# Decoder block in float32: attention's maxima and exponentials head by head, and the last batch's output bias on GpSimd

## The chip, the cores and the metric

The kernel runs on one core of a Trainium2 chip. The metric is the device time of one execution in microseconds (us). The kernel before has a median of 809.09 us over three runs (807.49 to 811.71). The engines are PE (TensorE), DVE (VectorE), ACT (ScalarE), POOL (GpSimd) and SP (SyncE, which only issues DMAs here).

## The reference

Input `x` is 4 batches of 512 tokens by 512 features. Three pre-norm layers follow, each added to its input:

```
x = x + attention(layernorm(x))     # 16 heads of 32, window of 128 keys, 4 sink keys
x = x + experts(layernorm(x), ids)  # 4 experts picked by token id
x = x + ffn(layernorm(x))           # ternary weights, 8-bit activations
# attention, per head:
scores = q @ k.T * HEAD_DIM ** -0.5, -inf where (j >= 4) & (j < i - 128)
probs  = softmax(scores)
out    = (probs @ v) @ Wo.T + bo
```

Only attention is touched by the change. There is no causal mask: a query row sees the sink keys, the 128 keys before it and all keys after it.

## The kernel before

Three phases run one after the other, with a barrier of all engines between them: attention (to about 456 us), experts (to about 600 us), feed-forward (to the end).

In attention the 16 heads go in 4 groups of 4 (`GH` = 4), the queries of a batch in 4 tiles of 128. A **unit** is one head group `g` of one query tile `qt`, written (g,qt) here; there are 64. The units of group 0 of the next batch are numbered (4,qt), so the program runs (0,0) to (0,3) of batch 0, then for each batch (1,0) to (4,3), and for the last batch (1,0) to (3,3). Every unit needs:

- scores of 4 heads, each in a bank of its own of `s_ps`, 512, 512, 388 or 260 keys wide for `qt` = 0 to 3 (L902), and for `qt` > 0 a matmul per head that adds the window's mask (L910). They wait until all four exponentials of the unit before are done, since they overwrite `s_ps`
- the negated maximum of each head's row, on DVE (`maxima`, L696): two instructions for two heads each
- the exponentials with their row sums, on ACT (`exps`, L527): one instruction per head
- four "slots" of transposes on PE (L930; L926 for the sink columns; L923 for the widened reciprocals of the sums in `qt` = 3). Slots 0 and 2 are copied out of PSUM by ACT (L539), slots 1 and 3 by DVE (L717, L714). There is one PSUM bank for each of the two engines, so slot 2 waits for ACT's copy of slot 0, and slot 3 for DVE's copy of slot 1
- after each second unit the product with V (`attend_pair`, L952, L944).

Every engine has its order written out by hand (`unit` of each engine). In unit u, PE first computes the scores of unit u+1, then slots 0 and 1 of u, then a piece of "side" work (12 matmuls of 512 columns, L843: a tile of the next Q, K, V or of the output projection), then slots 2 and 3. DVE in unit u takes the maxima of u+1, then copies slot 1, does its part of the side work, and copies slot 3. ACT copies slot 0, takes the exponentials of u+1, copies slot 2. In the last batch there is no side work left after group 1, except three pieces of output projection in (3,2) and (3,3).

POOL widens the reciprocals (`widen`, L391), splits the group's result into two parts (`split`, L399 and L402), loads the residual `xres`, adds the bias `bo` to it (`add_bo`, L443, one instruction of 2048 columns after `split(b, 2)`), and in the last batch splits the experts' weights (`expert_hi` L431, `expert_lo` L437). In the last batch DVE adds `bo`, in four instructions of 512 columns (L768) at the ends of the units of `BO_UNITS`: (2,1), (2,2), (2,3), (3,0).

## Time and profile before

| | before |
|---|---|
| three runs | 807.49, 809.09, 811.71 us |
| profiled execution | 808.96 us, of which the span of its instructions is 807.1 us |
| busy over the span | PE 92%, DVE 73%, ACT 59%, POOL 35% |
| instructions in all | 14098 |
| maxima (L696) on DVE | 128 instructions, 124.5 us |
| exponentials (L527) on ACT | 256 instructions, 152.3 us, and 52.8 us of accumulator reads |

A busy share is the time in which the engine had an instruction under way; an engine can be idle much of the time and still be the one that others wait for in a given stretch. "Idle before" an instruction is the gap on its engine, with the instruction that ended it.

### The profile page before, as it was taken

Reading aid. Unit: us, or ns where it says so; the run is one execution under the profiler, and the core shown is the slowest. Engines: PE = TensorE matmul, PEld = TensorE weight load, DVE = VectorE, ACT = ScalarE, POOL = GpSimd, SP = SyncE. Lnnn points to the kernel's source line nnn. Section 1 sums busy time; section 2 is a strip of 40 time slices with the busy share of each in tenths; the row PEclk is TensorE's granted clock in tenths of the full one; section 3 lists DMA queues with packets and bytes.
Section 4 is the critical chain, followed back from the end, with each engine's and each line's share of the span. In section 5 each row is a group of like instructions: output and inputs, shape, how many; then the busy total and the mean of one; then the engine's idle time right before and its main releaser. Section 6 shows DMA issues by size and latency. Waiting matters only on the chain. (4 is left out here: it accounts for less than half of the span.)

```text
span 807.1 us, 14098 instructions
## 1 busy us (share of the span) xinstructions
PE 740.2 (92%) x5150; PEld 507.8 (63%) x5150; DVE 590.4 (73%) x1092; ACT 473.2 (59%) x1025; POOL 281.0 (35%) x282
## 2 busy tenths in 40 slices
PE   5988999999999999999978789999957899999997
PEld 4756777777777777777655568888833343434443
DVE  6886666877668866677675467778628888888875
ACT  5555676666666666677555144444415766767674
POOL 2011213223042130314455234443214555555552
PEclk9998999999999999999989899999989999999999
DMA  9200031113121040313210375553122232433332
GB/s 312 107 1 28 27 105 37 45 54 131 52 81 54 28 157 27 106 30 129 105 53 2 95 274 176 201 199 137 46 82 85 52 85 73 105 91 73 73 78 79
DMA packets 56482, 74.12 MB, mean 92 GB/s; under 512 B 35615, under 2 KB 37663, under 8 KB 54752
## 3 DMA queue, kind: packets, MB, share of 16 engines
q1 hardware_dynamic: 50672, 56.17, 22.8%
q0 software_dynamic: 5456, 16.53, 5.9%
q8 instruction: 43, 0.70, 0.4%
q10 hardware_dynamic: 288, 0.52, 0.2%
q14 instruction: 23, 0.19, 0.1%
HBM read 52.71 MB, written 13.39 MB: 82 GB/s over the span
## 5 line engine op out<-in xcount | busy, mean ns | idle before, releaser
L527 ACT ACTIVATE probs<-s_ps,neg_max 128x512 f32<-128x512 f32 (+2 forms) x256 | 152.3, 610 | 19.5 <-DVE neg_max L696 18.1
L696 DVE TENSOR_REDUCE neg_max<-s_ps 128x2 f32<-128x1024 f32 (+2 forms) x128 | 124.5, 1014 | 33.6 <-PE s_ps L910 33.0
L930 PE MATMUL pT_ps<-ident,probs 128*128 128x128 f32 x832 | 115.6, 280 | 9.7 <-DVE probs L717 8.4
L539 ACT ACTIVATE probs<-pT_ps 128x512 f32<-128x512 f32 x96 | 57.4, 598 | 98.6 <-PE pT_ps L930 98.3
L930 PEld LDWEIGHTS pT_ps<-ident,probs 128*128 128x128 f32 x832 | 93.9, 144 | 25.2 <-DVE probs L717 11.2
L717 DVE COPY probs<-pT_ps 128x512 f32<-128x512 f32 x112 | 76.6, 684 | 36.8 <-PE pT_ps L930 36.5
L1473 POOL TENSOR_TENSOR hw<-h,ln_w_sb 128x512 f32<-128x512 f32 x64 | 83.2, 1310 | 52.3 <-DVE h L1606 52.3
L1738 PE MATMUL f_y_ps<-w_tern,hqT 128*128 128x512 bf16 x256 | 65.1, 379 | 11.8 <-DVE xn L1648 5.3
L1717 PE MATMUL gate_ps<-w_tern,xqT 128*128 128x512 bf16 x256 | 65.9, 380 | 8.3 <-DVE h L1606 7.4
L843 PE MATMUL side_ps<-w_hi 128*128 128x512 f32 x172 | 71.0, 413 | 0.0
L843 PE MATMUL side_ps<-w_hi,w_lo 128*128 128x512 f32 x172 | 67.3, 391 | 0.0
L843 PE MATMUL side_ps<-w_lo,w_hi 128*128 128x512 f32 x172 | 67.2, 391 | 0.0
L1717 PE MATMUL up_ps<-w_tern,xqT 128*128 128x512 bf16 x256 | 65.7, 379 | 0.0
L399 POOL TENSOR_TENSOR aT_hi<-norm,one_col 128x512 fp32r<-128x512 f32 x15 | 15.6, 1040 | 125.0 <-DVE norm L708 86.6
L1606 DVE SCALAR_TENSOR_TENSOR h<-up_ps,gu_scale,f_gate 128x512 f32<-128x512 f32 x64 | 47.7, 745 | 7.1 <-ACT f_gate L1529 7.0
L527 ACT ACTIVATION_READ_ACCUMULATOR probs<-s_ps,neg_max 128x1 f32 x256 | 52.8, 206 | 0.0
L952 PE MATMUL pv_ps<-probs,v_sb 128*32 128x256 f32 (+1 forms) x896 | 52.3, 369 | 0.2 <-ACT probs L539 0.2
L391 POOL TENSOR_TENSOR norm<-rinv,one_col 128x512 f32<-128x512 f32 x16 | 16.7, 1041 | 102.8 <-DVE rinv L703 102.8
L1717 PEld LDWEIGHTS gate_ps<-w_tern,xqT 128*128 128x128 bf16 x256 | 23.6, 98 | 42.0 <-DVE h L1606 15.4
L1738 PEld LDWEIGHTS f_y_ps<-w_tern,hqT 128*128 128x128 bf16 x256 | 23.2, 97 | 42.0 <-DMA hqT<-hq 18.0
L1522 ACT ACTIVATE hq<-hq_big,minus_offset 128x1024 bf16<-128x1024 f16 x30 | 34.3, 1143 | 25.4 <-DVE hq_big L1643 25.4
L1529 ACT ACTIVATE f_gate<-gate_ps,gu_scale 128x512 f32<-128x512 f32 x64 | 43.1, 674 | 8.2 <-PE gate_ps L1717 8.2
(247 smaller groups left out, 1635.5 us busy)
## 6 DMA issues: line engine op xcount, KB each, us to landing
w_piece<-w_ffn SPq DMA_DIRECT2D x24, 512.0 KB
w_stage<-w_ffn SPq DMA_DIRECT2D x12, 1024.0 KB
xres<-x POOLq DMA_DIRECT2D x4, 1024.0 KB, 5.7
xn<-x SPq DMA_DIRECT2D x12, 256.0 KB, 3.0
xn<-x SPq DMA_DIRECT2D x3, 1024.0 KB
x<-xres POOLq DMA_DIRECT2D x3, 1024.0 KB, 4.8
xn<-c SPq DMA_DIRECT2D x2, 1024.0 KB, 6.1
v_next<-c SPq DMA_DIRECT2D x2, 1024.0 KB, 6.0
```

The source lines that it names most:

```text
L527: nc.scalar.activation(weights[qt][:, h, at:at + width(qt)], s_ps[:, h, 0:width(qt)], ACT.Exp, bias=neg_max[:, qt % 2, h:h + 1], accum_out ...
L539: nc.scalar.activation(out, turned_p, ACT.Identity).then_inc(slot_copied[0], 1)
L696: nc.vector.tensor_reduce(neg_max[:, qt % 2, 2 * s:2 * s + 2], s_ps[:, 2 * s:2 * s + 2, 0:width(qt)], AX.X, ALU.max, negate=True).then_inc ...
L717: nc.vector.tensor_copy(weights[qt][:, :, a:z], pT_ps[:, 1, :].rearrange("p (h n) -> p h n", h=GH))\
L843: last = nc.tensor.matmul(out, lt, r, start=(first and n == 0), stop=(final and n == len(terms) - 1))
L930: last = nc.tensor.transpose(pT_ps[:, k % 2, h * P:h * P + P], weights[qt][:, h, a:z], ident[:])
L952: last = nc.tensor.matmul(pv_ps[HD * h:HD * h + HD, to], v_sb[:, slot, f:f + HD], p, start=first, stop=final, tile_position=(0, HD * h))
L1473: nc.gpsimd.tensor_tensor(hw[:, t % 2, c, :], h[:, t % 2, c, :], ln_w[:, c * CHK:c * CHK + CHK], ALU.mult)\
L1529: nc.scalar.activation(gate[:, c % 2, :], gate_ps[c % 2][:], ACT.Silu, scale=gu_scale[:, t % 2, 0:1])\
L1606: nc.vector.scalar_tensor_tensor(h[:, i, c, :], up_ps[c % 2][:], gu_scale[:, i, 1:2], gate[:, c % 2, :], ALU.mult, ALU.mult).then_inc(h_re ...
L1717: last = nc.tensor.matmul(out[:], xqT[:, t % 2, k, :], weights[:, k, cols], start=(k == 0), stop=(k == DK - 1))
L1738: last = nc.tensor.matmul(y_ps[:], hqT[:, t % 2, k, :], down_w[:, k, :], start=(k == 0), stop=(k == FK - 1))
```

## The change

`maxima` issues four instructions for one head each instead of two for two heads, and each waits for its own head's scores; PE signals after every head; each exponential waits for its own head's maximum. In the last batch the bias is added on POOL by one instruction of 2048 columns between `widen(b, 2)` and `split(b, 2)`, and DVE's four additions go.

```
-BO_UNITS = [(2, 1), (2, 2), (2, 3), (3, 0)]
...
                 widen(b, 2)
+                add_bo(b)
                 split(b, 2)
...
-                def exps(b, g, qt, s):
-                    act.wait_ge(max_ready, units_before(b, g, qt) * 2 + s + 1)
+                def exps(b, g, qt):
                     at = BAND - width(qt) if qt >= 2 else 0
-                    for h in (2 * s, 2 * s + 1):
+                    for h in range(GH):
+                        act.wait_ge(max_ready, units_before(b, g, qt) * GH + h + 1)
                         nc.scalar.activation(weights[qt][:, h, at:at + width(qt)], s_ps[:, h, 0:width(qt)], ACT.Exp,
...
-                def maxima(b, g, qt, s):
-                    dve.wait_ge(scores_ready, units_before(b, g, qt) * 2 + s + 1)
-                    nc.vector.tensor_reduce(neg_max[:, qt % 2, 2 * s:2 * s + 2], s_ps[:, 2 * s:2 * s + 2, 0:width(qt)],
-                                            AX.X, ALU.max, negate=True).then_inc(max_ready, 1)
+                def maxima(b, g, qt):
+                    for h in range(GH):
+                        dve.wait_ge(scores_ready, units_before(b, g, qt) * GH + h + 1)
+                        nc.vector.tensor_reduce(neg_max[:, qt % 2, h:h + 1], s_ps[:, h, 0:width(qt)], AX.X, ALU.max, negate=True)\
+                            .then_inc(max_ready, 1)
...
-                    if last and (g, qt) in BO_UNITS:
-                        t = BO_UNITS.index((g, qt))
-                        if t == 0:
-                            dve.wait_ge(xres_loaded, (b + 1) * 16)
-                        nc.vector.tensor_tensor(xres[:, t, :], xres[:, t, :], bo_sb[:], ALU.add).then_inc(bo_added, 1)
...
                                                     start=(n == 0), stop=(n == 2 and not masked), tile_position=(HD * h, 0))
+                            if n == 2 and not masked:
+                                last.then_inc(scores_ready, 1)
                     if not masked:
-                        last.then_inc(scores_ready, 2)
                         return
...
                     for h in range(GH):
-                        last = nc.tensor.matmul(s_ps[:, h, at + free:at + P], ident_bf[:], window_mask[:, free:P], start=False, stop=True)
-                        if h % 2:
-                            last.then_inc(scores_ready, 1)
+                        nc.tensor.matmul(s_ps[:, h, at + free:at + P], ident_bf[:], window_mask[:, free:P], start=False, stop=True)\
+                            .then_inc(scores_ready, 1)
```

The callers call `maxima` and `exps` once instead of twice.

DVE in the last batch, from the end of unit (2,0) to the middle of (2,3), before (`neg_max` are the maxima, `probs<-pT_ps` a slot's copy, `xres<-xres,bo_sb` the bias):

```order
L717 COPY probs<-pT_ps 128x4x128 [waits slot_transposed] x2
L768 TENSOR_TENSOR xres<-xres,bo_sb 128x512 [waits xres_loaded]
L696 TENSOR_REDUCE neg_max<-s_ps 128x2 [waits scores_ready] x2
L743 TENSOR_REDUCE sinks<-probs 128x16 [waits exp_done]
L717 COPY probs<-pT_ps 128x4x128 [waits slot_transposed] x2
L768 TENSOR_TENSOR xres<-xres,bo_sb 128x512
L703 RECIPROCAL rinv<-sums 128x16 [waits rinv_widened,exp_done]
L696 TENSOR_REDUCE neg_max<-s_ps 128x2 [waits scores_ready] x2
```

and in the changed kernel:

```order
L716 COPY probs<-pT_ps 128x4x128 [waits slot_transposed] x2
L695 TENSOR_REDUCE neg_max<-s_ps 128x1 [waits scores_ready] x4
L741 TENSOR_REDUCE sinks<-probs 128x16 [waits exp_done]
L716 COPY probs<-pT_ps 128x4x128 [waits slot_transposed] x2
L702 RECIPROCAL rinv<-sums 128x16 [waits rinv_widened,exp_done]
L695 TENSOR_REDUCE neg_max<-s_ps 128x1 [waits scores_ready] x4
```

The additions no longer stand between a unit's last copy and the next maxima, and each group of maxima has four rows' worth of instructions instead of two.

POOL in the last batch, before (`norm<-rinv` is `widen`, `aT_hi` and `aT_lo` are `split`, `w_hi` and `w_lo` the experts' weights):

```order
L431 TENSOR_TENSOR w_hi<-xn,one_col 128x2048 [waits side_done,c_loaded2]
L391 TENSOR_TENSOR norm<-rinv,one_col 128x512 [waits attn_split,rinv_ready]
L399 TENSOR_TENSOR aT_hi<-norm,one_col 128x512 [waits attn_ready]
L402 TENSOR_TENSOR aT_lo<-norm,aT_hi 128x512 [waits attn_hi_ready]
L437 TENSOR_TENSOR w_lo<-xn,w_hi 128x2048 [waits c_split]
L431 TENSOR_TENSOR w_hi<-v_next,one_col 128x2048 [waits side_done,c_loaded3]
```

and in the changed kernel:

```order
L430 TENSOR_TENSOR w_hi<-xn,one_col 128x2048 [waits side_done,c_loaded2]
L390 TENSOR_TENSOR norm<-rinv,one_col 128x512 [waits attn_split,rinv_ready]
L442 TENSOR_TENSOR xres<-xres,bo_sb 128x2048 [waits xres_loaded,wide_bias_loaded]
L398 TENSOR_TENSOR aT_hi<-norm,one_col 128x512 [waits attn_ready]
L401 TENSOR_TENSOR aT_lo<-norm,aT_hi 128x512 [waits attn_hi_ready]
L436 TENSOR_TENSOR w_lo<-xn,w_hi 128x2048 [waits c_split]
L430 TENSOR_TENSOR w_hi<-v_next,one_col 128x2048 [waits side_done,c_loaded3]
```

One instruction is added, between the widening and the split.

## Rows read from the trace of the kernel before

**Rows 1.** Stages: start:end, length, busy us (instructions) by engine, PE clock, DMA
```profile
92.00:398.00 306.00, 304.10 (x2686) 232.35 (x2688) 214.80 (x340) 205.52 (x562) 85.16 (x66) 1.00 0.23 75
398.00:456.00 58.00, 45.92 (x406) 31.55 (x395) 38.75 (x53) 25.23 (x75) 25.84 (x11) 0.94 0.12 41
```

**Rows 2.** Waits of PE, 92 to 398 us: total us, times, longest
```profile
PE pT_ps L930 <- DVE probs L717: 0.6, 2, 0.3
```

**Rows 3.** Waits of PE, 398 to 441 us
```profile
PE pT_ps L930 <- DVE probs L717: 5.3, 5, 1.7
PE pT_ps L926 <- DVE sinks L743: 2.6, 2, 1.9
```

**Rows 4.** Order of time, DVE and PE, unit (4,3) of batch 1: start, us, instruction
```profile
264.35 2.28 DVE L696 TENSOR_REDUCE neg_max<-s_ps 128x2 f32<-128x1024 f32 x2
266.56 0.16 DVE L743 TENSOR_REDUCE sinks<-probs 128x16 f32<-128x16 f32 x1
266.63 0.68 DVE L717 COPY probs<-pT_ps 128x512 f32<-128x512 f32 x1
...
267.44 0.60 PE L923 MATMUL pT_ps<-ident,norm 128*128 128x128 f32 x4
```

**Rows 5.** Order of time, DVE: two statistics of 512 columns, back to back
```profile
148.57 1.27 DVE L588 BATCH_NORM_STATS2 bn_st<-xn 128x6 f32<-128x512 f32 x2
```

**Rows 6.** Groups by form, DVE: count, busy us, mean ns, idle before
```profile
L588 DVE BATCH_NORM_STATS2 bn_st<-xn 128x6 f32<-128x512 f32 x12 | 7.7, 679 | 0.0
L768 DVE TENSOR_TENSOR xres<-xres,bo_sb 128x512 f32<-128x512 f32 x4 | 6.3, 1578 | 0.0
```

**Rows 7.** Waits of PE, 33 to 92 us
```profile
PE pT_ps L926 <- DVE sinks L743: 3.0, 1, 3.0
```

**Rows 8.** Order of time, units (2,1) and (2,2) of the last batch
```profile
410.04 3.59 POOL L431 TENSOR_TENSOR w_hi<-xn,one_col 128x2048 fp32r<-128x2048 f32 x1
...
410.31 3.87 DVE L768 TENSOR_TENSOR xres<-xres,bo_sb 128x512 f32<-128x512 f32 x1
...
412.42 0.40 PE L910 MATMUL s_ps<-window_mask,ident_bf 128*128 128x128 bf16 x4
...
413.30 0.60 ACT L539 ACTIVATE probs<-pT_ps 128x512 f32<-128x512 f32 x1 [2.59 <-PE pT_ps L930]
414.10 1.29 DVE L696 TENSOR_REDUCE neg_max<-s_ps 128x2 f32<-128x520 f32 x2
414.82 0.48 ACT L527 ACTIVATE probs<-s_ps,neg_max 128x260 f32<-128x260 f32 x1 [0.93 <-DVE neg_max L696]
```

**Rows 9.** PE in unit (2,3), last batch; then the stage's windows row
```profile
418.29 1.97 PE L930 MATMUL pT_ps<-ident,probs 128*128 128x128 f32 x8
416.80:420.30 3.50, 3.34 (x20) 2.31 (x20) 3.36 (x5) 0.96 (x3) 1.04 (x1) 0.56 0.00 0
```

**Rows 10.** Order of time, units (3,0) and (3,1) of the last batch
```profile
424.84 1.04 PE L930 MATMUL pT_ps<-ident,probs 128*128 128x128 f32 x8
...
429.84 1.08 DVE L768 TENSOR_TENSOR xres<-xres,bo_sb 128x512 f32<-128x512 f32 x1
...
430.84 1.82 DVE L696 TENSOR_REDUCE neg_max<-s_ps 128x2 f32<-128x776 f32 x2
...
431.83 0.58 ACT L527 ACTIVATE probs<-s_ps,neg_max 128x388 f32<-128x388 f32 x1 [0.50 <-DVE neg_max L696]
```

**Rows 11.** Order of time, POOL: the bias of batch 2, then the last batch
```profile
329.80 4.59 POOL L443 TENSOR_TENSOR xres<-xres,bo_sb 128x2048 f32<-128x2048 f32 x1
...
418.35 1.04 POOL L391 TENSOR_TENSOR norm<-rinv,one_col 128x512 f32<-128x512 f32 x1 [4.72 <-DVE rinv L703]
427.96 1.04 POOL L399 TENSOR_TENSOR aT_hi<-norm,one_col 128x512 fp32r<-128x512 f32 x1 [8.58 <-DVE norm L708]
...
441.29 1.04 POOL L391 TENSOR_TENSOR norm<-rinv,one_col 128x512 f32<-128x512 f32 x1 [2.42 <-DVE rinv L703]
```

**Rows 12.** Waits of ACT, 92 to 398 us
```profile
ACT probs L527 <- DVE neg_max L696: 11.7, 22, 0.7
```

More of the change, by code:

```diff
@@ L545, in unit @@
                     if more:
-                        exps(b, *nxt, 0)
-                        exps(b, *nxt, 1)
+                        exps(b, *nxt)
                     copy_slot(b, g, qt, 2)
@@ L560, in unit @@
                                              accum_out=abs_sum[:, n, bass.ds(b, 1)]).then_inc(piece_done, 1)
-                exps(0, 0, 0, 0)
-                exps(0, 0, 0, 1)
+                exps(0, 0, 0)
                 for qt in range(TT):
@@ L732, in unit @@
                     if more:
-                        maxima(b, *nxt, 0)
-                        maxima(b, *nxt, 1)
+                        maxima(b, *nxt)
                     if qt == 0 and 0 < g < HG:
@@ L804, in experts_of_tiles @@
                     then(nc.vector.tensor_scalar(expert_of[:], expert_f[:], float(DK), None, ALU.mult))
-                maxima(0, 0, 0, 0)
-                maxima(0, 0, 0, 1)
+                maxima(0, 0, 0)
                 dve.wait_ge(wide_bias_loaded, 32)
```

## The prediction, made before the changed kernel ran

> **What bounds the kernel now.** I read the stages first. From 92 to 398 us, batches 0 to 2 and group 1 of the last, PE is busy 304.1 of 306.0 us [rows 1]: PE is the bound there, and its waits for DVE's slot copies come to 0.6 us [rows 2]. What DVE and ACT gain or lose in that stretch counts only where it is more than the time by which they are early. From 398 to 456 us, the units of the last batch without side work, PE is busy 45.9 of 58.0 us [rows 1], and in the first 43 us of these it waits 5.3 us for DVE's slot copies and 2.6 us for the sink columns [rows 3], both of which stand behind the maxima in DVE's order. The same waits stand in batch 0's first groups: one of 3.0 us for the sink columns [rows 7]. So the change can be felt in two short stretches; the experts and the feed-forward (after 456 us) have the same code and only move along.
>
> **Maxima of one head, the cost.** Two maxima of 2 x 512 columns occupy DVE for 2.21 us, from 264.35 to the start of the next instruction at 266.56 [rows 4]. No maximum over one head stands in the trace. The nearest instruction is one of 512 columns on DVE: two statistics take 1.27 us together and 0.68 us each [rows 5, 6], so one starts 0.59 us after the other. Four of these are 2.38 us: **+0.17 us per unit**. The lower bound is +0 (the columns are the same), the upper is no overlap at all, 4 x 0.68 = 2.72 us, +0.51 us per unit. I take 0.17, since back-to-back instructions are what the change makes, and keep both ends. The Trainium skill speaks against the split: "VectorE: DVE Perf Modes", section on the TRN2 errata, gives a fixed 120 cycles for each instruction that reads PSUM and says that many small tiles pay it each. By that figure two more instructions cost 0.25 us per unit, and my sum would come out about 1.5 us higher.
>
> **Where that lands.** With a mask, the first maximum now starts after one mask matmul instead of two, about 0.1 us earlier (four take 0.40 us) [rows 8], which leaves +0.06 us. Without one (the maxima in qt = 3, of the next unit's qt = 0), DVE is late already when it starts them, so the full 0.17 counts. In (4,3) the copy behind them ends at 266.63 + 0.68 = 267.31 and PE's transposes that need it start at 267.44 [rows 4], 0.13 us later; about 0.06 of that is what passes even where PE waits, so 0.07 us is to spare and 0.10 us is lost. I looked at this gap in every unit: three units (4,3) lose 0.10 each, the seven others of qt = 3 about 0.02 each, that is 0.45 us; (4,1) of batches 0 and 1, where PE waits already [rows 2], lose 0.17 each, 0.34 us; of batch 0's first groups [rows 7] two or three units lose 0.17 each, 0.4 us; (2,0) and (3,0) of the last batch 0.06 each, 0.1 us. Together **+1.3 us**.
>
> **Exponentials per head, the gain.** ACT waits for a maximum 22 times in the PE-bound stretch, 11.7 us in all [rows 12], and each wait shrinks by about 0.5 us, the half of the two-head maximum that is no longer waited for. But PE needs the exponentials only behind its side work, and none of PE's waits there is for them [rows 2]; I cost it at nothing, covered by PE's side matmuls. In the last batch ACT is mostly held by its own copy of slot 0 before the exponentials, not by the maxima, so an earlier first maximum changes nothing there either. ACT does not starve later: one head's exponential is 0.6 us on average (152.3 us for 256 in the table above), and DVE's step is at most 0.59.
>
> **The bias leaves DVE.** This is the gain. Its four additions take 6.3 us, 1578 ns on average [rows 6], though a free one takes 0.68 us. The first lasts 3.87 us, from 410.31, beside POOL's 3.59 us instruction from 410.04, and ends with it; the next maxima start at 414.10, though their scores' masks were done by 412.8 [rows 8]. The Trainium skill says this of that row: "SBUF — State Buffer", section on who interferes with whom, has a DVE instruction with two SBUF inputs and a GpSimd instruction that reads SBUF exclude each other for the whole instruction. The trace agrees, 3.87 us for a 0.68 us addition.
> Without it the maxima start at about 412.7, the exponentials right after ACT's copy (413.30 + 0.60) at 413.9 instead of 414.82 [rows 8], the sink columns and slot 3 1.3 us earlier; the later of the two sets the next scores, **-1.1 us**.
> In (2,3) the eight transposes take 1.97 us, and 1.04 us in (3,0) [rows 9, 10], because PE runs at 0.56 of full clock from 416.8 to 420.3, close to the lower of its two levels (1.2 and 2.4 GHz) [rows 9], after 1.9 and more us idle. With the gap filled I expect the full clock and **-0.8 us**; the bounds are 0 (the clock falls all the same) and -1.5 (a second such stretch at the last batch's start goes too).
> In (3,1) the last addition takes 1.08 us and holds the maxima to 430.84 and the exponentials 0.50 us [rows 10]: **-0.5 us**. The two others lie beside waits of DVE and cost nothing.
>
> **The bias on POOL.** One instruction, 4.59 us in batch 2 [rows 11]. It starts when the widening ends, 418.35 + 1.04 = 419.4, and ends at 424.0; the split behind it waits for DVE's product until 427.96 [rows 11], so it is hidden with 4 us to spare. Nothing on DVE in that time has two SBUF inputs (maxima and copies read PSUM), so the 3.87 us case does not recur. If the cover were gone, the split and the experts' halves behind it would be late, and next the last widening, which had 2.42 us to spare [rows 11]. PE waits for this bias only in the final projection.
>
> **Sum.** 1.3 - 1.1 - 0.8 - 0.5 = -1.1 us against the profiled execution's 808.96 us (span 807.1 us and 1.9 us around it), which is 0.1 us under the median of 809.09: **807.9 us**.
>
> **The rivals.**
> *The single maxima cost their full duration* (slower). Then every unit takes 0.51 us more DVE time. What is over the gap in front of slot 3: nine units of qt = 3 lose 0.35 to 0.45 us, 3.8 in all, the three (2,0) units of the middle batches 0.15 each, (4,1) 0.5 twice, the first groups 1.5, the last batch 0.8: +7.6 us against +1.3, and 808.96 + 7.6 - 2.4 = 814.2 us. It decides from about 0.35 us per unit. For it: the gap is only 0.07 to 0.16 us in qt = 3. Against it: the 0.59 us between two statistics [rows 5].
> *The filled gaps return more* (faster). If both slow-clock stretches go (-1.5 instead of -0.8) and the early exponentials let PE's last groups run 0.3 to 0.5 us shorter in each of the six units without side work, the sum is 1.3 - 1.1 - 1.5 - 0.5 - 2.4 = -4.2: 804.8 us. For it: PE waits 8 us there [rows 3]. Against it: ACT's copy holds the exponentials in those units.
> *The removed addition is no gain*, because something else (ACT's exponentials, or the clock) holds (2,2) and (2,3) as long. Then 0.3 to 0.5 us is won and 1.3 lost: 809.8 us. For it: DVE's waits move easily to ACT, which ends 0.9 us behind it there [rows 8].
>
> **How the numbers follow.** A measurement of this kernel tells about 0.5%, 4 us, from no change. Forecast 0.62; the removed addition is no gain 0.18; single maxima at full price 0.08; more returned 0.12. The third rival and the forecast lie within 0.5%; the faster rival lies just at the bound, so I count it faster for most of its chance: faster 0.12, same 0.80, slower 0.08. The range takes in the faster rival's end and the third rival with the skill's price on top, not the slow one: 804.6 to 811.0 us.
>
> **What would show it.** Right: about 0.6 us between starts of single maxima; about 1 us or less of new PE waits from 92 to 398 us; the maxima of (2,3) starting 0.1 us after their masks begin; POOL's bias near 4.6 us, ended some us before the split; attention's end about 1 us earlier, and the later phases' lengths unchanged. Wrong: a pitch of 0.68 us with PE waits on slot copies in every qt = 3; the POOL bias longer because it is locked out by DVE; or PE still at the low clock around (2,3).

## The result: 0.57% slower, and the profile after

| | before | changed |
|---|---|---|
| median, 13 runs each | 809.61 us (807.49 to 811.71) | 812.89 us (811.58 to 816.29) |
| ratio to before, 95% interval | 1 | 1.0057 (1.0042 to 1.0072) |
| profiled execution | 808.96 us, span 807.1 | 812.39 us, span 810.5 |
| granted TensorE clock over the span | 0.983 | 0.977 |
| instructions | 14098 | 14224 |

The forecast was 807.9 us, in 804.6 to 811.0. The kernel is slower than that range allows. In the changed kernel the maxima are L695, the exponentials L527, a slot's transposes L922 (L918 the sinks, L915 the reciprocals), DVE's copies L716 and L713, the scores L894, the mask L903, POOL's bias L442.

First DVE, where the prediction expected its price. The groups by form of the changed kernel (line, engine, operation, shapes, count, busy us, mean ns, idle before), then in order of time unit (4,3) of batch 1, which answers to [rows 4]:

```profile
L695 DVE TENSOR_REDUCE neg_max<-s_ps 128x1 f32<-128x512 f32 x128 | 78.5, 676 | 14.2 <-PE s_ps L903 13.4 <-PE s_ps L894 0.4
```

```profile
264.80 2.41 DVE L695 TENSOR_REDUCE neg_max<-s_ps 128x1 f32<-128x512 f32 x4
267.13 0.16 DVE L741 TENSOR_REDUCE sinks<-probs 128x16 f32<-128x16 f32 x1
267.21 0.68 DVE L716 COPY probs<-pT_ps 128x512 f32<-128x512 f32 x1
...
267.94 0.66 PE L915 MATMUL pT_ps<-ident,norm 128*128 128x128 f32 x4
```

One maximum alone takes 676 ns, but four back to back take 2.41 us, where two of two heads took 2.28: **+0.13 us per unit** (0.17 was forecast, the full-duration rival had 0.51). The copy now ends at 267.89 and PE's transposes that need it start at 267.94, 0.05 us later. The distance was 0.13 us before: PE had that little to spare, and now starts them as soon as the copy is passed on.

Next the waits, in two stretches of PE and one of ACT (total us, times, longest), against [rows 2, 3, 12]. PE from 92 to 398 us, then PE from 398 to 441 us, then ACT from 92 to 398 us:

```profile
PE pT_ps L922 <- DVE probs L716: 0.9, 2, 0.5
PE pT_ps L915 <- POOL norm L390: 0.8, 2, 0.6
```

```profile
PE pT_ps L922 <- DVE probs L716: 4.6, 4, 1.8
PE pT_ps L918 <- DVE sinks L741: 2.3, 2, 1.7
```

```profile
ACT probs L527 <- DVE neg_max L695: 1.3, 6, 0.2
```

ACT's wait for the maxima shrank from 11.7 to 1.3 us, and PE gained nothing by it. PE's waits in the last batch went from 5.3 + 2.6 to 4.6 + 2.3 us. By the waits alone the kernel should be about as fast as before.

The stages (start:end, length, busy us and instructions of PE, PE's loads, DVE, ACT, POOL, then the granted clock) show what waits don't. Of the changed kernel:

```profile
92.00:398.00 306.00, 303.57 (x2664) 231.26 (x2662) 219.58 (x433) 204.29 (x561) 84.41 (x65) 1.00 0.22 75
398.00:456.00 58.00, 47.08 (x416) 32.16 (x414) 34.36 (x63) 25.09 (x75) 30.66 (x12) 0.94 0.11 37
422.00:425.40 3.40, 3.40 (x34) 2.06 (x26) 0.30 (x1) 0.00 (x0) 0.87 (x1) 0.50 0.02 5
...
456.00:480.00 24.00, 16.82 (x68) 13.52 (x69) 10.12 (x25) 5.36 (x8) 9.78 (x14) 0.72 0.74 259
```

and the same start of the experts in the kernel before:

```profile
456.00:480.00 24.00, 18.01 (x85) 14.91 (x86) 12.11 (x30) 7.59 (x10) 9.92 (x15) 0.86 0.72 252
```

The experts' code is the same in both, yet in these 24 us PE got through 68 instructions instead of 85, at a clock of 0.72 instead of 0.86. One of its matmuls in each kernel, in order of time, the changed one first:

```profile
467.57 0.63 PE L1288 MATMUL e_z_ps<-w_lo,e_xT_hi 128*128 x1
```

```profile
466.84 0.40 PE L1296 MATMUL e_z_ps<-w_lo,e_xT_hi 128*128 x1
```

Of the 3.4 us between these two profiled executions, 0.5 are there when the experts start (457.4 against 456.9), 2.9 by PE's transposes behind these matmuls (472.26 against 469.40), and 2.7 when the feed-forward's first statistics start (605.5 against 602.8). But two profiles are one draw each of a clock that differs from execution to execution, so the experiments had to say what belongs to the change; the 2.2 us that the experts take longer here are not in the second profile of the changed kernel (see the stages under "The low clock").

The additions and POOL, in order of time, against [rows 8, 11]:

```profile
410.92 3.60 POOL L430 TENSOR_TENSOR w_hi<-xn,one_col 128x2048 fp32r<-128x2048 f32 x1
...
413.28 0.40 PE L903 MATMUL s_ps<-window_mask,ident_bf 128*128 128x128 bf16 x4
...
413.55 1.44 DVE L695 TENSOR_REDUCE neg_max<-s_ps 128x1 f32<-128x260 f32 x4 [2.49 <-PE s_ps L903]
414.16 0.60 ACT L539 ACTIVATE probs<-pT_ps 128x512 f32<-128x512 f32 x1 [2.59 <-PE pT_ps L922]
414.65 0.47 ACT L527 ACTIVATE probs<-s_ps,neg_max 128x260 f32<-128x260 f32 x1
...
418.34 4.53 POOL L442 TENSOR_TENSOR xres<-xres,bo_sb 128x2048 f32<-128x2048 f32 x1
429.07 1.04 POOL L398 TENSOR_TENSOR aT_hi<-norm,one_col 128x512 fp32r<-128x512 f32 x1 [6.20 <-DVE norm L707]
```

The maxima start with their masks, the exponentials right behind ACT's copy, and POOL's bias takes 4.53 us and ends 6.20 us before the split: all as forecast. What came of it for PE stands in its rows of (2,3) and of the next scores:

```profile
417.64 1.09 PE L922 MATMUL pT_ps<-ident,probs 128*128 128x128 f32 x8
...
421.50 1.92 PE L944 MATMUL pv_ps<-probs,v_sb 128*32 128x256 f32 x24
...
423.36 0.80 PE L894 MATMUL s_ps<-k_hi,q_hi 32*128 32x512 f32 x3
```

The eight transposes run at full clock now, 1.09 us instead of 1.97 [rows 9]. But the clock fell 4.8 us later, from 422.0 to 425.4 us, where PE has its product and the scores of (3,1) to do instead of transposes between waits.

### The profile page after: what moved, and what is told of

The parts are those of the page before. It is cut to its first block and busy times, and to the rows that moved or that the text cites. A ratio compares the mean times of both kernels' runs of the same rounds, so it can differ in the third digit from the quotient of the medians.

```text
span 810.5 us, 14224 instructions
## 1 busy us (share of the span) xinstructions
PE 744.9 (92%) x5150; PEld 510.2 (63%) x5150; DVE 592.2 (73%) x1216; ACT 472.3 (58%) x1025; POOL 285.5 (35%) x283
## 5 line engine op out<-in xcount | busy, mean ns | idle before, releaser
L695 DVE TENSOR_REDUCE neg_max<-s_ps 128x1 f32<-128x512 f32 (+2 forms) x256 | 132.8, 581 | 37.1 <-PE s_ps L903 36.3
L527 ACT ACTIVATE probs<-s_ps,neg_max 128x512 f32<-128x512 f32 (+2 forms) x256 | 152.4, 613 | 4.0 <-DVE neg_max L695 3.5
L922 PE MATMUL pT_ps<-ident,probs 128*128 128x128 f32 x832 | 114.7, 278 | 9.5 <-DVE probs L716 8.2
L922 PEld LDWEIGHTS pT_ps<-ident,probs 128*128 128x128 f32 x832 | 93.4, 143 | 24.6 <-DVE probs L716 11.0
L716 DVE COPY probs<-pT_ps 128x512 f32<-128x512 f32 x112 | 76.7, 685 | 35.3 <-PE pT_ps L922 35.0
L835 PE MATMUL side_ps<-w_lo,w_hi 128*128 128x512 f32 x172 | 67.1, 390 | 0.0
L527 ACT ACTIVATION_READ_ACCUMULATOR probs<-s_ps,neg_max 128x1 f32 x256 | 53.5, 209 | 0.0
```

Source lines behind the costliest of these rows:

```text
L527: nc.scalar.activation(weights[qt][:, h, at:at + width(qt)], s_ps[:, h, 0:width(qt)], ACT.Exp, bias=neg_max[:, qt % 2, h:h + 1], accum_out ...
L695: nc.vector.tensor_reduce(neg_max[:, qt % 2, h:h + 1], s_ps[:, h, 0:width(qt)], AX.X, ALU.max, negate=True)\
L716: nc.vector.tensor_copy(weights[qt][:, :, a:z], pT_ps[:, 1, :].rearrange("p (h n) -> p h n", h=GH))\
L835: last = nc.tensor.matmul(out, lt, r, start=(first and n == 0), stop=(final and n == len(terms) - 1))
L922: last = nc.tensor.transpose(pT_ps[:, k % 2, h * P:h * P + P], weights[qt][:, h, a:z], ident[:])
```

## The experiments

Two theories to begin with: the head-by-head maxima cost it, or the bias on GpSimd does. Then: is it DVE's time, the order of the exponentials, or the clock.

All runs in one table. "Low clock" is worked out for each execution as its time x (1 - granted clock) x 2, since the two levels are 1.2 and 2.4 GHz; means with their standard errors, of 12 executions each (9 of split_pair_wait). Ratios are to runs of the kernel before on the same chip, with the 95% interval. The first result's 13 executions of the changed kernel have a mean of 813.8 ± 0.5 us and 37.3 ± 0.9 us at the low clock.

| kernel | median us | ratio | mean us | low clock, us |
|---|---|---|---|---|
| before_again | 809.29 | 0.9999 (0.9985 to 1.0013) | 809.4 ± 0.3 | 27.4 ± 0.9 |
| after_again | 812.72 | 1.0045 (1.0029 to 1.0060) | 813.0 ± 0.3 | 33.2 ± 1.2 |
| heads_only | 814.50 | 1.0061 (1.0036 to 1.0086) | 814.9 ± 1.0 | 39.7 ± 1.7 |
| bo_pool_only | 809.88 | 1.0010 (0.9988 to 1.0033) | 810.5 ± 0.8 | 32.2 ± 1.3 |
| split_pair_wait | 817.08 | 1.0071 (1.0045 to 1.0096) | 815.7 ± 0.9 | 36.3 ± 1.2 |
| before_fill | 812.24 | 1.0038 (1.0021 to 1.0054) | 812.6 ± 0.5 | 24.0 ± 1.4 |
| bo_pool_fill | 812.26 | 1.0031 (1.0010 to 1.0052) | 812.0 ± 0.5 | 22.2 ± 1.6 |
| after_fill | 812.48 | 1.0039 (1.0020 to 1.0059) | 812.9 ± 0.6 | 19.3 ± 1.8 |
| bo_pool_fill_early | 809.87 | 1.0000 (0.9985 to 1.0015) | 810.0 ± 0.5 | 24.4 ± 1.0 |
| after_fill_early | 809.38 | 1.0001 (0.9988 to 1.0015) | 809.9 ± 0.4 | 24.0 ± 1.2 |
| heads_with_side | 812.34 | 1.0039 (1.0021 to 1.0058) | 812.5 ± 0.8 | 34.8 ± 1.9 |
| heads_without_side | 811.05 | 1.0011 (0.9998 to 1.0023) | 810.5 ± 0.4 | 31.9 ± 1.2 |
| unmasked_heads | 812.01 | 1.0023 (1.0003 to 1.0043) | 811.6 ± 0.7 | 34.0 ± 2.1 |
| masked_heads | 811.65 | 1.0021 (0.9998 to 1.0044) | 810.5 ± 0.8 | 29.2 ± 2.2 |
| pairs_two_tiny | 812.45 | 1.0050 (1.0031 to 1.0069) | 813.2 ± 0.6 | 34.7 ± 1.5 |

The kernel before itself, in the 131 executions that these ratios go by, has a mean of 809.5 ± 0.1 us and 30.2 ± 0.4 us at the low clock.

### The two halves of the change

**heads_only**: the change with the bias back on DVE.

```
+BO_UNITS = [(2, 1), (2, 2), (2, 3), (3, 0)]
...
-                add_bo(b)
...
+                    if last and (g, qt) in BO_UNITS:
...
+                        nc.vector.tensor_tensor(xres[:, t, :], xres[:, t, :], bo_sb[:], ALU.add).then_inc(bo_added, 1)
```

> Maxima and exponentials go head by head; the last batch's bias stays on DVE. Theory A (the extra DVE time is small and the rest of the slowdown is where PE's low-clock stretches fall): 1 to 2 us over the kernel before, since from 86 to 399 us the changed kernel lost 1.1 us, and mean granted clocks that vary from run to run as much as those of the kernel before. Theory B (head by head costs what was measured, the bias is neutral): 3.5 to 5 us over the kernel before.

**bo_pool_only**: the other half, two-head maxima and exponentials per pair as before, the bias on POOL.

```
-BO_UNITS = [(2, 1), (2, 2), (2, 3), (3, 0)]
...
+                add_bo(b)
...
-                    if last and (g, qt) in BO_UNITS:
```

> Two-head maxima as before; only the last batch's bias moves to POOL. Theory A: 1 to 2.5 us under the kernel before, (2,1) to (2,2) of the last batch 1.1 us or more shorter, the last addition's 0.5 us gone. Theory C (the move of the bias brings the low-clock stretches that the changed kernel shows at 422 to 425 us and at the start of the experts, and so costs): 2 to 4 us over the kernel before, with a second low-clock stretch after the experts' start.

heads_only is 0.61% slower, bo_pool_only is not told from the kernel before (+0.10%, -0.12 to +0.33), which fits neither of its two expectations. **The head-by-head part costs the time, and the bias on GpSimd gives back none that these runs can tell.**

**after_again** and **before_again** are the two kernels unchanged, with profiles of their own.

> The changed kernel once more, to see which of its low-clock stretches recur. Theory A: the stretches lie elsewhere than at 422.0 and 466.4 us in this profile, and the time is 1 to 5 us over the kernel before, by run. Theory B or C: the same two stretches recur within a few us, and the time is 3 to 5 us over the kernel before.

> The kernel before once more, as the measure of what means nothing. Both theories: within 0.1 % of itself. Theory A: its granted clocks by run spread as widely as those of the changed kernel (0.973 to 0.980), and its profile may have a second low-clock stretch at the experts' start. Theories B and C: its clocks stay at 0.98 or above and only one such stretch of 6.8 us lies at the experts' start.

The second profile of the kernel before weakens one step of the prediction. In order of time:

```profile
412.04 1.03 DVE L768 TENSOR_TENSOR xres<-xres,bo_sb 128x512 f32<-128x512 f32 x1
412.48 4.05 POOL L431 TENSOR_TENSOR w_hi<-xn,one_col 128x2048 fp32r<-128x2048 f32 x1
```

The addition that took 3.87 us beside POOL's instruction [rows 8] takes 1.03 us here, because it started 0.44 us before POOL's and not 0.27 us after it; POOL's took 4.05 us instead of 3.59. The Trainium skill has this in "SBUF — State Buffer", section on who interferes with whom: the order of issue decides which of the two is blocked. Both traces agree on the order. They don't on the winner's price: DVE's addition was first here and took 0.35 us more than a free one all the same. The last addition of the kernel before shows it again: from 429.84 us, 0.48 us ahead of a POOL instruction, it takes 1.08 us [rows 10]. Of the four profiles with the bias on DVE and no matmuls added to PE, three (before, heads_only, split_pair_wait) have the long one, 3.84 to 3.87 us, and before_again the short one. In these three, unit (2,2) takes 4.9 to 5.1 us, in before_again 4.0. So the prediction priced the row rightly, but the kernel before doesn't pay it in every execution; how often it does, two profiles of it can't say.

The lengths of PE's units in the last batch, each from the start of its first scores to the start of the next unit's, in us:

| unit | before | before_again | bo_pool_only | after | after_again |
|---|---|---|---|---|---|
| (2,1) | 7.0 | 6.8 | 7.2 | 7.3 | 7.1 |
| (2,2) | 5.1 | 4.0 | 4.0 | 4.0 | 4.0 |
| (2,3) | 6.4 | 5.9 | 5.9 | 6.6 | 7.1 |
| (3,0) | 5.8 | 5.8 | 5.8 | 6.9 | 6.5 |
| (3,1) | 6.7 | 6.7 | 6.5 | 6.1 | 6.1 |

In (2,2) 1.0 of the forecast's 1.1 us is won against the one profile and nothing against the other. In (3,1) 0.6 us are won (0.5 forecast). The profile of bo_pool_only has 3.4 us at the low clock in this unit, from 430.1 us; in pairs_two_tiny (below), which has the bias on POOL and two-head maxima and no low clock there, the unit takes 6.1 us too, so it is the removed addition that wins them, not the early exponentials. In (2,3) and (3,0) both profiles of the changed kernel are longer, by the low clock that now falls there (422.0 to 425.4, and 3.4 us from 423.7 in after_again).

### DVE's time or the exponentials' order

**split_pair_wait**: heads_only, but the exponentials wait for the second maximum of each pair.

```
-                        act.wait_ge(max_ready, units_before(b, g, qt) * GH + h + 1)
+                        if h % 2 == 0:
+                            act.wait_ge(max_ready, units_before(b, g, qt) * GH + h + 2)
```

> One-head maxima, the bias on DVE, but an exponential waits for both maxima of its pair. Theory A' (the longer DVE work costs, not the earlier exponentials): as head by head alone, 3.5 to 6 us over the kernel before. Theory E (the earlier exponentials cost, by ending ACT's work sooner and leaving longer idle or other collisions): 0 to 2 us over the kernel before.

Its ACT waits again for the maxima (92 to 398 us), as before the change [rows 12]:

```profile
ACT probs L528 <- DVE neg_max L696: 13.4, 25, 0.7
```

and it is 0.71% slower, a little more than heads_only (0.61%, intervals overlapping). The early exponentials are not the cost; if anything they give a little back.

**pairs_two_tiny** turned this round, at the end: two-head maxima, all signals as before, the bias on POOL, and two additional 4-column maxima per unit that nobody reads.

```
+                    nc.vector.tensor_reduce(scrap[:, units_before(b, g, qt), s:s + 1], s_ps[:, 2 * s, 0:4], AX.X, ALU.max, negate=True)
                     nc.vector.tensor_reduce(neg_max[:, qt % 2, 2 * s:2 * s + 2], s_ps[:, 2 * s:2 * s + 2, 0:width(qt)],
```

> The bias is on GpSimd and the maxima stay two-head, but before each of them DVE takes one more maximum, of 4 columns of the same scores into a place that nobody reads: two more PSUM-reading instructions per unit, no other order and no signal of a head. If it is DVE's time alone that slows the kernel, the two instructions add 0.1 to 0.2 us per unit (0.065 us each is what a split added) and the time is 0.3 to 0.7% over the kernel before, with the scores of (1,3) of batch 0 to the last batch 0.8 us or more longer. If it is the signals or the order of the single heads, the time stays within 0.15% of it.

Unit (4,3) of batch 1 again, in order of time:

```profile
267.26 0.10 DVE L697 TENSOR_REDUCE scrap<-s_ps 128x1 f32<-128x4 f32 x1
267.28 1.21 DVE L698 TENSOR_REDUCE neg_max<-s_ps 128x2 f32<-128x1024 f32 x1
268.40 0.15 DVE L697 TENSOR_REDUCE scrap<-s_ps 128x1 f32<-128x4 f32 x1
268.47 1.21 DVE L698 TENSOR_REDUCE neg_max<-s_ps 128x2 f32<-128x1024 f32 x1
...
269.68 0.68 DVE L719 COPY probs<-pT_ps 128x512 f32<-128x512 f32 x1
```

From the first of these to the copy it is 2.42 us, as in the changed kernel (2.41), against 2.28 before: two instructions that do next to no work cost 0.14 us. The kernel is 0.50% slower (0.31 to 0.69), which is the whole slowdown, with 34.7 us at the low clock. **DVE's added time alone is enough for it**, without the signals per head and without another order of the exponentials.

### How much of it is plain lateness

From the scores with which PE's unit (1,3) of batch 0 begins to those of (1,3) of the last batch are 48 units of the PE-bound stretch. PE runs at full clock in nearly all of it, and the length varies little between profiles. The rows of PE's scores in order of time, of the kernel before:

```profile
78.74 0.51 PE L902 MATMUL s_ps<-k_hi,q_hi 32*128 32x512 f32 x4
...
392.09 0.51 PE L902 MATMUL s_ps<-k_hi,q_hi 32*128 32x512 f32 x4
```

of the changed one:

```profile
78.64 0.51 PE L894 MATMUL s_ps<-k_hi,q_hi 32*128 32x512 f32 x4
...
392.84 0.51 PE L894 MATMUL s_ps<-k_hi,q_hi 32*128 32x512 f32 x4
```

and of pairs_two_tiny:

```profile
80.79 0.51 PE L899 MATMUL s_ps<-k_hi,q_hi 32*128 32x512 f32 x4
...
395.28 0.51 PE L899 MATMUL s_ps<-k_hi,q_hi 32*128 32x512 f32 x4
```

That is 313.35, 314.20 and 314.49 us. The second profiles give 313.4 (before_again) and 314.2 (after_again), bo_pool_only 313.4. heads_only has 314.3. So **0.85 us** is lateness in the steady stretch, present in each profile of the changed kernel.

To see which units bring it, the changed kernel with head-by-head maxima in a part of its units only (`by_head` picks them, the others have two-head maxima and exponentials that wait for a pair):

```
+        def by_head(b, g, qt):
+            return qt == 0
...
+                        act.wait_ge(max_ready, units_before(b, g, qt) * GH + (h + 1 if by_head(b, g, qt) else h // 2 * 2 + 2))
...
+                    if not by_head(b, g, qt):
+                        for h in (0, 2):
```

**unmasked_heads** has `qt == 0`, **masked_heads** `qt > 0`.

> The bias is on GpSimd; the maxima go head by head only for qt = 0 (16 of 64 units, 512 columns and no mask, taken in the qt = 3 units where DVE has least time to spare); the other 48 units have two maxima of two heads. Theory A (the slowdown is DVE's lateness, where it is late): all of the steady 0.8 to 0.9 us between the scores of (1,3) of batch 0 and the last batch's start comes back here, and the time lies 0.3 to 0.6% over the kernel before, as with all units. Theory B (every unit's single maxima add to it, through the many short gaps of PE and its low clock): a quarter to a third of the slowdown, 0.1 to 0.2%.

> The complement: head by head for qt = 1 to 3, two-head maxima for qt = 0. Theory A: the steady part is at most 0.1 us, 0.0 to 0.15% over the kernel before, with the low clock's share (about 30 us per run) as in the kernel before. Theory B: two thirds to three quarters of the slowdown, 0.3 to 0.45%, and 34 us or more of low clock per run.

The same two rows of scores in them:

```profile
80.34 0.51 PE L903 MATMUL s_ps<-k_hi,q_hi 32*128 32x512 f32 x4
...
394.14 0.50 PE L903 MATMUL s_ps<-k_hi,q_hi 32*128 32x512 f32 x4
```

```profile
78.83 0.51 PE L903 MATMUL s_ps<-k_hi,q_hi 32*128 32x512 f32 x4
...
392.53 0.51 PE L903 MATMUL s_ps<-k_hi,q_hi 32*128 32x512 f32 x4
```

That is 313.80 and 313.70 us: 0.45 and 0.35 us over the kernel before, 0.80 together. Theory A, with all of it in the unmasked units, is refuted. Taken unit by unit, in the same way as the table of the last batch (length of PE's unit less its length in the profile of before, us; all changes over 0.1):

| PE's unit | unmasked_heads | masked_heads | after | after_again | pairs_two_tiny |
|---|---|---|---|---|---|
| (1,3), batch 0 | -0.22 | 0 | -0.22 | -0.22 | 0.07 |
| (4,1), batches 0 and 1, each | 0 | 0.13, 0.12 | 0.13 | 0.13 | 0.13 |
| (4,3), batches 0, 1, 2, each | 0.12 | 0 | 0.11 to 0.13 | 0.12 to 0.13 | 0.12 to 0.14 |
| (1,3), batch 1 | 0.27 | 0.05 | 0.29 | 0.28 | 0.29 |

These are the units that the prediction named, (4,3) and (4,1), with 0.12 and 0.13 us where it had 0.10 and 0.17, and one that it had at 0.02. They come to 0.7 us; the rest of the 0.85 lies in changes of under 0.1 us. The times of the two kernels, +0.23% and +0.21% with intervals from about 0 to 0.44%, do not decide between the theories.

### The low clock

0.85 us is a quarter of the slowdown at most. The four kernels with single maxima in every unit (after, after_again, heads_only, split_pair_wait; 46 executions) have a mean of 814.2 ± 0.4 us and 36.6 ± 0.7 us at the low clock. Against the 131 of the kernel before that is +4.8 us of time and +6.4 us at the low clock; for the 25 executions of the changed kernel alone it is +3.9 ± 0.3 and +5.1 ± 0.9 us.

What a microsecond at the low clock costs is not one number. Within heads_only and within bo_pool_only the time rises by 0.5 us for each, within the three kernels run last by 0.30 to 0.35, within the 131 executions of the kernel before by 0.14, and within after, after_again and before_again by less than 0.1. before_again has 3.3 us less of it than the kernel before in the same session, at the same time. With 0.14 to 0.5 us for each, an estimate, 0.9 to 3.2 of the 4.8 us go with the clock.

The profiles say where it costs. The lengths of five stages (us), parted at the scores at 78.74 and 392.09 us above, at PE's first matmul into `e_y_ps`, and at DVE's first `f_bn_st`:

| stage | before | before_again | bo_pool_only | after | after_again | heads_only | split_pair_wait | pairs_two_tiny |
|---|---|---|---|---|---|---|---|---|
| start | 78.7 | 81.1 | 80.4 | 78.6 | 80.7 | 83.6 | 82.8 | 80.8 |
| 48 steady units | 313.35 | 313.4 | 313.4 | 314.2 | 314.2 | 314.3 | 314.5 | 314.5 |
| last batch | 67.4 | 65.2 | 65.3 | 67.1 | 67.2 | 68.9 | 67.8 | 66.1 |
| experts | 143.3 | 143.5 | 143.1 | 145.5 | 143.2 | 144.7 | 143.0 | 144.3 |
| feed-forward | 204.3 | 204.4 | 204.9 | 205.1 | 205.1 | 204.9 | 204.8 | 204.9 |

The two last borders in order of time, of the kernel before and of the changed one:

```profile
459.47 4.62 PE L1310 MATMUL e_y_ps<-ident 128*128 128x128 f32 x20
...
602.76 0.69 DVE L1568 BATCH_NORM_STATS2 f_bn_st<-xn 128x6 f32<-128x512 f32 x1 [8.67 <-DMA xn<-x]
```

```profile
459.96 3.90 PE L1302 MATMUL e_y_ps<-ident 128*128 128x128 f32 x20
...
605.47 0.69 DVE L1560 BATCH_NORM_STATS2 f_bn_st<-xn 128x6 f32<-128x512 f32 x1 [8.40 <-DMA xn<-x]
```

The last five kernels of the table, those with DVE's added time in every unit, are longer than the mean of the first three by 1.2, 0.9, 1.5, 0.9 and 0.4 us: the most of it lies in attention, not in the experts, and each profile is one draw.

- **Start.** The very first scores begin anywhere from 24.0 to 26.3 us, before any maximum, so a part of this row is no effect of the change. From there to the stage's end, the three profiles with the low clock in the same two places (from about 58 and 72 us) take 56.1 (bo_pool_only), 56.6 (pairs_two_tiny) and 56.7 us (after_again): about 0.5 us of lateness in the first groups.
- **Last batch.** In each of these five profiles, and in unmasked_heads, the clock falls at 422.0 to 423.7 us, where PE has its product to do. None of the six other profiles without added matmuls has it there (417.2 in before, 430.1, 429.2 and 430.4 in bo_pool_only, heads_with_side and heads_without_side, nowhere from 411 to 456 in before_again and masked_heads). (bo_pool_fill_early, with matmuls added, has it at 422.4 us with two-head maxima.) The changed kernel's 67.1 and 67.2 us stand against 65.3 for bo_pool_only, which has as much low clock 6 to 8 us later. The windows of 3.4 us of after_again and bo_pool_only (busy us and instructions of PE first, the granted clock third from the end):

```profile
423.70:427.10 3.40, 3.40 (x37) 1.99 (x37) 0.69 (x1) 0.18 (x2) 1.32 (x1) 0.50 0.02 5
```

```profile
430.10:433.50 3.40, 3.40 (x17) 2.66 (x15) 2.39 (x3) 2.59 (x8) 3.40 (x2) 0.50 0.00 0
```

- **Experts.** Over all 17 profiles (code and work are the same), the nine with 9.7 to 10.4 us at the low clock take 142.9 to 143.5 us, the eight with 11.1 to 16.4 take 144.3 to 146.1: about 0.4 us for each microsecond.
- **Feed-forward.** It has 0.8 to 7.7 us at the low clock and takes 203.9 to 205.5 us, with no relation between the two.

To test it, I filled PE's idle time: six matmuls of 512 columns into a free bank between slots 2 and 3 of each unit without side work.

```
+                    if not name and not (last and g == HG - 1 and qt >= 2):
+                        fill(b)
...
+                    for n in range(FILL):
+                        nc.tensor.matmul(side_ps[:], w_hi["o"][:, 0, 0:P], w_hi["o"][:, 0, :], start=True, stop=True)
```

This is in **before_fill**, in **after_fill**, and in **bo_pool_fill** (bo_pool_only with it).

> The kernel before, with six matmuls of 512 columns into an unused bank between the third and fourth transposes of each unit without side work (batch 0's three, the last batch's six); their results are overwritten unread. Theory A (half of PE's low-clock time is lost, and the low clock in attention comes from PE's idle gaps): the low-clock stretches in attention mostly go, the mean granted clock rises by 0.006 or more, 3 to 6 us under the kernel before. Theory D (the stretches don't depend on these gaps): clock unchanged, time the same or up by what the fill delays.

> The changed kernel with the same fill. Theory A: the difference to the filled kernel before shrinks from about 4 us to the steady part, 0.9 to 1.5 us less what the moved bias gives, so between 0 and 1.5 us slower than it, and faster than the kernel before by 2 to 5 us. Theory B (head by head costs 4 us whatever the clock does): still 3.5 to 5 us over the filled kernel before.

> Two-head maxima, the bias on POOL, and the fill: the candidate to beat both. Theory A: 1 to 2.5 us under the filled kernel before, since with the clock held the removed addition's 1.1 and 0.5 us in the last batch are seen; 4 to 8 us under the kernel before. Theory D: the same as the bias on POOL alone.

All three are equally slow, 0.31 to 0.39%, where their theories A had 2 to 8 us gained over the kernel before. The fill takes 7 to 16 us out of the low clock and costs more in itself than it saves, but no difference between the kernels can be told any more: after_fill over before_fill is 0.4 us in the means (812.9 and 812.6, ± 0.8 for the difference), with 4.7 ± 2.3 us less at the low clock.

**bo_pool_fill_early** and **after_fill_early** fill only where `qt` is 0 or 1, the units without sink columns:

```
-                    if not name and not (last and g == HG - 1 and qt >= 2):
+                    if not name and qt < 2:
```

> Two-head maxima, the bias on POOL, and the six filling matmuls only in units of qt 0 and 1 (batch 0's (1,0), (1,1), the last batch's (2,0), (2,1), (3,0), (3,1)), where PE waits 1.3 to 1.8 us for slot 1 anyway; in the first fill they also stood in front of the sink columns' units and held slot 3 up. Theory A: 2 to 5 us under the kernel before, clock up by 0.004 or more. If the fill in itself costs (its matmuls run into the attention product's time), the same as the kernel before.

> The changed kernel with the same early fill. Theory A: 0.5 to 1.5 us over the kernel with two-head maxima and this fill. Theory B: 3 us or more over it.

Windows of the last batch, 398 to 456 us, the changed kernel with the early fill, then its twin with two-head maxima:

```profile
398.00:456.00 58.00, 50.55 (x449) 35.68 (x447) 35.51 (x66) 26.81 (x82) 30.98 (x12) 1.00 0.15 51
```

```profile
398.00:456.00 58.00, 52.24 (x450) 36.70 (x448) 34.66 (x52) 27.73 (x84) 30.98 (x12) 0.97 0.12 42
```

Both have the time of the kernel before (1.0001 and 1.0000), and 24 us at the low clock each. With PE kept busy there, the change costs nothing that can be measured: the early fill takes 3.5 us off the changed kernel (means of 813.4 over its 25 executions and 809.9) and 0.5 off the other. The steady lateness is still in its trace, the same units by the same 0.12 and 0.13 us. No version beats the kernel before. One rival is left: the fill stands where PE waits for DVE's copies, so it can also hide DVE's lateness in those units, and no run holds the clock without filling the waits. Against it, head-by-head maxima in the 10 units around these waits alone cost nothing (heads_without_side, next).

**heads_without_side** and **heads_with_side** asked where the extra low clock comes from: head-by-head maxima only in the 10 units whose maxima are not taken beside side work (and the bias on POOL), or only in the 54 others.

```
+            return u in (4, 5, 6) or u >= (BATCH - 1) * GU + 2 * TT + 1
```

> The bias on POOL; head by head only for the 10 units whose maxima lie where PE has no side work. Theory A: 1.5 to 3 us over the kernel with the bias on POOL alone, with 3 to 6 us more low-clock time. Theory B: within 0.7 us of it.

> The bias on POOL; head by head only for the 54 units whose maxima lie beside PE's side work, two heads at once for the 10 others. Theory A (of the changed kernel's 3 to 4 us, about 1 is DVE time over the gaps in the PE-bound stretch and the rest comes from more low-clock time in the units where PE idles): 0.5 to 1.5 us over the kernel with the bias on POOL alone, that is 810 to 811.5 us, low-clock time like that kernel's (32 us). Theory B (the cost is spread over all units, in the PE-bound stretch too): 2 to 3 us over it.

I had expected the larger part from the 10 units where PE has gaps. It was the other way round: over bo_pool_only the 10 units have 0.0 ± 0.9 us in the means, the 54 have 2.0 ± 1.1. The 48 steady units take 313.36 us in heads_without_side and 314.16 in heads_with_side, so the steady lateness is all in units with side work.

## Why the prediction was wrong, point by point

- **Single maxima, +0.17 us per unit: right in kind, 0.13 measured.** The row of statistics that it rested on [rows 5, 6] was the right neighbour (four starts 0.59 us apart are 2.36 us, so these rows give 0.15, not 0.17). By the Trainium skill's 120 cycles ("VectorE: DVE Perf Modes", the TRN2 errata) it would have been 0.25, an estimate; the trace has about 0.07 us for each instruction added back to back.
- **Where that lands, +1.3 us: right in size, nearly right in place.** The forecast had 0.45 + 0.34 us for the steady stretch, the traces have 0.85: (4,3) three times 0.12, (4,1) twice 0.13, (1,3) of batch 1 0.29 instead of 0.02, and (1,3) of batch 0 a gain of 0.22. The first groups have about 0.5 us where it had 0.4. The 0.1 us of the last batch can't be read out, since the low clock moves that stretch by more.
- **Exponentials per head, nothing: right.** ACT's wait went from 11.7 to 1.3 us and bought nothing that can be told; split_pair_wait, without that gain, is 0.1% slower than heads_only, with intervals that overlap.
- **The bias leaves DVE, -1.1 us: this step failed as a gain over the kernel's executions.** The price is right where the long addition occurs (4.9 to 5.1 us for (2,2), 4.0 without it), but before_again doesn't have it, and bo_pool_only gains nothing that can be told. Nor did that addition end with POOL's instruction, as the prediction says: it ended at 414.18 us, POOL's at 413.63.
- **PE at full clock in (2,3), -0.8 us: this step failed.** The transposes did shrink, 1.97 to 1.09 us, but the low clock came 5 us later, on more work: (2,3) and (3,0) take 13.5 us in both profiles of the changed kernel, 12.2 and 11.8 before. The range for this term ended at 0, "the clock falls all the same"; a loss was not in it.
- **(3,1), -0.5 us: right**, 0.6, and by the removed addition.
- **The bias on POOL, hidden: right**, 4.53 us (4.59 forecast), ended 6.20 us before the split.
- **"The experts and the feed-forward have the same code and only move along": this step failed too.** Their code is the same, their clock is not. The sum had no term for the clock but a gain. The experts take 2.2 us more in the one profile of the changed kernel and nothing more in the other, the feed-forward 0.7 in both.
- **The rivals.** The slow one (full price of 0.51 us per unit) came near the time, 814.2 us, by a mechanism that the trace rules out. "The removed addition is no gain", 809.8, had the right idea of the bias and no idea of the clock.

Set against the profile that it started from, the forecast had +0.4, +0.8, -2.3, 0 and 0 us for the five stages, and the profile after has -0.1, +0.85, -0.3, +2.2 and +0.7 (after_again +2.0, +0.9, -0.2, -0.1 and +0.7). The steady part was right; what failed in both is the last batch's gain, and beyond it the assumption that the clock does the same elsewhere. With 1.4 for the lateness, -0.5 for (3,1), nothing for the other gains and the experts' 0.4 us for each of the 5.1 us more at the low clock, the sum from 809.5 is 812.4 us by an estimate; the mean of the 25 executions of the changed kernel is 813.4. That last microsecond has no account.

**What stays open.** That DVE's added time is enough for the whole slowdown is shown (pairs_two_tiny). That it works through the clock is shown less well: the low clock of pairs_two_tiny is 5.2 ± 1.7 us over the kernel before in its session but only 2.6 ± 2.0 over bo_pool_only, and after_again has 2.5 ± 1.5 over its session's. The fill removes the difference, but fills waits as well. Which of PE's gaps tip the clock isn't known: splitting the units by side work put the cost on those with side work, splitting them by mask left it undecided, and one kernel's executions spread by 5 us and more. The fall at 422.0 to 423.7 us goes with single or added maxima in six of twelve profiles and is absent in the other six, which is an association of single draws. It is also argued, not shown, that the experts' extra low clock is brought about in attention; no run changed the phase between them.

## What to carry to other kernels

Where PE waits for a copy that stands behind DVE's work, splitting DVE's instructions costs even at 0.07 us each, so look first whether anybody needs the earlier result: here ACT's wait for it, 11.7 us in the list of waits, cost PE nothing. Count a gain from a row of one profile (a 3.87 us addition, a stretch at the low clock) only after a second profile has it too. And where a kernel has PE near idle in places, ask of each added delay what it does to the clock there and in the phases behind it, in executions by the dozen and not in one trace.

## What the runs showed of the hardware

- Two PSUM-reading DVE instructions more per unit cost 0.13 to 0.14 us, whether they share the work (2.41 us for four) or do next to none (2.42 us with two of 4 columns), although such a small one takes 0.10 to 0.15 us by its own row.
- The time at TensorE's low clock differs between executions of one kernel by several microseconds (masked_heads took 806.1 us at a granted clock of 0.987 and 813.7 us at 0.977), and so does the start: PE's first four side matmuls of 512 columns take 1.19 us in the profile of before and 2.07 in that of the changed kernel, from the same code. The Trainium skill says this of the start ("TensorE: Matmul & The Clock Gate", Part 1): how many matmuls run slow at first varies from run to run of one kernel.
- A DVE addition of 0.68 us and a POOL instruction of 3.59 us that both read SBUF cost 0.35 and 0.46 us more when DVE's is first by 0.44 us, and 3.2 us more, all on DVE, when POOL's is first by 0.27 us.
- The same work at the low clock costs by where it falls: 0.4 us for each microsecond in the experts (17 profiles), nothing that shows in the feed-forward (0.8 to 7.7 us of low clock, 203.9 to 205.5 us).
